# Second layer of a two-layer graph network: counts gathered in pieces and turned by VectorE instead of TensorE, own rows gathered whole, and an edited front

## The reference

```python
h = relu(layernorm(x));  x = x + attention(h, src, dst, W, b_w, a, b_a)
h = relu(layernorm(x))
gates = softmax(h @ gate_W + gate_b);  top_v, top_i = top_k(gates, 2)
def sage_conv(h, W_l, b_l, W_r):
    aggr = segment_sum(h[src], dst) * inv_deg      # mean over a node's neighbours
    return aggr @ W_l + b_l + h @ W_r
for e in range(4):                                  # expert e
    he = relu(sage_conv(h, Wl[e, 0], bl[e, 0], Wr[e, 0]))
    out_e = relu(sage_conv(he, Wl[e, 1], bl[e, 1], Wr[e, 1]))
x = x + sum over the two best experts of gate * out_e
```

## Time and profile before

| | |
|---|---|
| median of 3 runs | 739.95 us (739.89 to 740.51) |
| the profiled execution | 741.92 us, its span 740.2 us |
| TensorE, share of the span | 97% |
| VectorE, ScalarE, GpSimd | 57%, 54%, 26% |
| chain that ended last | TensorE 90%, VectorE 5%, ScalarE 2% |

### The profile page before, as it was taken

How to read it: one execution, slowest core, us unless ns; L and a number is a source line. 1 busy time by engine, 2 the same in 40 slices (tenths; PEclk the granted TensorE clock), 3 DMA queues, 4 the chain that set the end, 5 groups by cost and what they waited for, 6 DMA issues and landing times.

```text
span 740.2 us, 12236 instructions
## 1 busy us (share of the span) xinstructions
PE 720.9 (97%) x3671; PEld 586.5 (79%) x3671; DVE 425.2 (57%) x1052; ACT 398.9 (54%) x898; POOL 191.3 (26%) x207
## 2 busy tenths in 40 slices
PE   7899999999999999999999999989999999999995
PEld 5698977888888888777777777878888888888884
DVE  7989889999752538622722622648345443453541
ACT  8866678776643521511511511347677675687761
POOL 4300000000000101850200010044566467556531
PEclk9999999999999999999999999999999999999998
DMA  9000001111501247799699595379844897327960
GB/s 214 34 4 3 4 3 30 40 35 36 169 4 58 84 125 242 217 334 323 238 354 322 199 363 192 100 191 265 295 93 85 210 292 225 75 73 190 286 203 14
DMA packets 46445, 115.21 MB, mean 156 GB/s; under 512 B 8340, under 2 KB 8552, under 8 KB 46361
## 3 DMA queue, kind: packets, MB, share of 16 engines
q1 hardware_dynamic: 28581, 77.60, 33.0%
q0 software_dynamic: 9136, 19.65, 11.5%
q10 hardware_dynamic: 8644, 16.86, 6.8%
HBM read 64.89 MB, written 50.08 MB: 155 GB/s over the span
## 4 chain that ended last, share of the span: by engine, by line
PE 90%; DVE 5%; ACT 2%; issue 1%; DVEq 0%; POOL 0%; ACTq 0%; POOLq 0%
PE ps L1814 16%; PE ps L1815 16%; PE ps L1816 16%; PE ps L2243 7%; PE ps L2242 6%; PE ps L2043 3%; PE ps L2037 3%; PE ps L2110 3%; PE ps L2111 3%; PE ps L2038 3%; DVE onehot_g L1325 3%; PE ps L1902 2%; PE ps L2173 2%; PE ps L1981 1%; PE ps L1983 1%
## 5 line engine op out<-in xcount | busy, mean ns | idle before, releaser
L1127 ACT ACTIVATE agn<-ps,rec 32x128 f32<-32x128 f32 x336 | 121.1, 361 | 33.3 <-PE ps L2243 18.8
L1055 ACT ACTIVATE slots<-he_t 125x512 fp32r<-125x512 f32 x40 | 25.4, 636 | 150.8 <-DVE he_t L1610 136.0
L2243 PE MATMUL ps<-slots,CTs 125*128 x230 | 90.0, 391 | 0.0
L1610 DVE TENSOR_TENSOR he_t<-ps,b_b 125x512 f32<-125x512 f32 x40 | 27.6, 691 | 105.7 <-PE ps L1816 72.5
L734 POOL DMA_INDIRECT hrow<-t_d,piece_i x80 | 76.1, 951 | 27.1 <-issue 23.8
L2242 PE MATMUL ps<-slots,CTs 125*128 x207 | 80.7, 390 | 0.3 <-issue 0.3
L1814 PE MATMUL ps<-W,agT_hi 128*125 128x512 f32 x160 | 63.5, 397 | 0.0
L1814 PE MATMUL ps<-W,h2T_hi 128*125 128x512 f32 x160 | 63.4, 396 | 0.0
L1816 PE MATMUL ps<-W,agT_lo 128*125 128x512 f32 x160 | 63.3, 396 | 0.0
L1815 PE MATMUL ps<-W,agT_hi 128*125 128x512 f32 x160 | 63.2, 395 | 0.0
L1815 PE MATMUL ps<-W,h2T_hi 128*125 128x512 f32 x160 | 63.2, 395 | 0.0
(11 more groups left out here) (335 smaller groups left out, 1716.8 us busy)
## 6 DMA issues: line engine op xcount, KB each, us to landing
he_d<-slots SPq DMA_DIRECT2D x30, 448.0 KB
slots<-he_d SPq DMA_DIRECT2D x30, 448.0 KB
w_d<-slots SPq DMA_DIRECT2D x3, 4096.0 KB, 17.7
slots<-w_d SPq DMA_DIRECT2D x24, 512.0 KB
t_d<-he_t SPq DMA_DIRECT2D x40, 224.0 KB
raw<-in_L_gnn_Wl ACTq DMA_DIRECT2D x4, 1024.0 KB, 8.9
raw<-in_L_gnn_Wr ACTq DMA_DIRECT2D x4, 1024.0 KB, 5.5
slots<-in_L_gnn_Wl ACTq DMA_DIRECT2D x4, 1024.0 KB, 9.4
```

The lines of the kernel that those rows point to most:

```text
L1127: last = a.activation(agn[32 * r:32 * r + 32, q, :], ps[n, 3 + i % 2, 128 * r:128 * r + 128], ACT.Copy, scale=rec[n, i, 4:5])
L2243: last = mm(o, CTs[:, t, :], part(k, P, t * 1024 + D, P), start=False, stop=t == T - 1)
```

## The change

Second step: the counts are written to `c_d` with permuted columns, 320 for each of four groups (32 nodes of each of ten tiles). `gather_counts` issues four indirect DMAs of 128 x 320 f16 by `piece_i`, and one VectorE transpose (`turn_counts`, 128 x 1,280 f16) puts the turned counts in `cth`; ScalarE copies them to `CTs` (`counts_in`, one instruction; three for tile 1). TensorE's `turn_rows` and VectorE's casts are gone. `gather_hidden` gathers whole rows for every tile, and `turn_hidden` is 16 instructions for every tile but the first. TensorE's turn of tile 0's own rows moves into the middle of `transformed(0)`.

Front: `W0_lo` is made by VectorE in the first batch, the rest of `a_sum` and `s_add` by GpSimd, and VectorE's flags of the second batch are loaded inside `sources`. `ident_a` and the rows 96 to 127 of `ct_16` are filled by GpSimd once the first products are done, and `counts_16(0)` on ScalarE waits for that.

```diff
 def gather_counts(i):                                   # GpSimd
-    gather(crow[i % 3][:], c_d, i, 0, crow_in[i % 3])
+    for q in range(RQ):
+        g.indirect_dma_start(crow[i % 3][:, q, :], None, c_d.rearrange("n (r f) -> (n r) f", r=RQ),
+                             bass.IndirectOffsetOnAxis(ap=piece_i[:, q, i:i + 1], axis=0)
+                             ).then_inc(crow_in[i % 3].sem, 16)
...
 def gather_hidden(i):
-    if i < HB:
-        gather(by_row(hrow[i]), t_d.rearrange("e p t d -> (e p t) d"), i, 1, hrow_in[i])
-        return
-    for q in range(RQ):
-        g.indirect_dma_start(hrow[i % HB][:, q, :], None, t_d.rearrange("e p t (r f) -> (e p t r) f", r=RQ),
...
+    gather(by_row(hrow[i % HB]), t_d.rearrange("e p t d -> (e p t) d"), i, 1, hrow_in[i % HB])
...
+def counts_in(i):                                       # ScalarE
+    if i > 0:
+        act.wait_ge(*agg_done(i))
+    act.wait_ge(*crow_turned(i + 1))
+    for r, n in enumerate(TURNS) if i == 1 else ((0, T),):
+        last = copy(CTs[:, 4 * r:4 * r + n, :], cth[0:P, 4 * r * S:(4 * r + n) * S].rearrange("p (t n) -> p t n", n=S))
...
                 mean_high(i)
+                if i + 2 < NT:
+                    counts_in(i + 2)
                 if i + 1 < NT - 1:
                     mean(i + 1)
...
-def counts_in(i):                                       # VectorE
+def turn_counts(i):
+    dve.wait_ge(*crow_in[i % 3](16 * RQ * (i // 3 + 1)))
     if i > 0:
-        dve.wait_ge(*agg_done(i))
-    for r, n in enumerate(TURNS):
-        dve.wait_ge(*crow_turned(3 * i + r + 1))
-        v.tensor_copy(CTs[:, 4 * r:4 * r + n, :], turned_counts(r, n)).then_inc(cts_ready.sem, 1)
+        dve.wait_ge(*cts_ready(3 * i))
+    v.transpose(cth[:].rearrange("p (t q c) -> p q t c", q=RQ, c=32),
+                crow[i % 3][:].rearrange("p q (t a) -> p q t a", a=32)).then_inc(crow_turned.sem, 1)
...
                 mean_low(i)
                 if i + 2 < NT:
-                    counts_in(i + 2)
+                    turn_counts(i + 2)
                 if i + 1 < NT:
                     turn_hidden(i + 1)
...
-            def turn_rows(i):                           # TensorE
...
-                if i + 2 < NT:
-                    turn_rows(i + 2)
...
+            def first_weights_low():                    # VectorE, in the first batch
+                dve.wait_ge(*w0_hi_ready(1))
+                v.tensor_tensor(W0_lo[:], W0_f[:], f32(W0_hi[:]), ALU.subtract).then_inc(w0_lo_ready.sem, 1)
```

More of the change, by code:

```diff
@@ L236, in gnn_kernel @@
         ag1 = at("ag1", [P, 4, D], F32, R4 + 8192)
[L237 to L241, removed]
+        c_nat = at("c_nat", [P, 2, N], F32, R3 + 21792)
+        ct_16 = [at(f"ct_16_{k}", [128, T, Q], F16, R3 + 4096 + 5024 * k) for k in range(2)]
+        c_16 = at("c_16", [P, 2, RQ * T * 32], F16, R3 + 14144)
+        c_lo = at("c_lo", [P, N], F16, R3 + 19264)
+        ident_a = at("ident_a", [128, 128], F16, R2 + 39328)
         slots = at("slots", [128, 2, 18432], F32R, 0)
@@ L663, in _ @@
                             pool.wait_ge(*ct_out(LOW_OUT, 64 * q + 32 * i))
-                        g.tensor_tensor(c_lo[:], c_nat[:, i, :], c_16[:, i, :], ALU.subtract
-                                        ).then_inc(rest_ready.sem, 1)
+                        low, nat = (o.rearrange("p (t n) -> p t n", n=P) for o in (c_lo[:], c_nat[:, i, :]))
+                        rounded = c_16[:, i, :].rearrange("p (r t a) -> p t r a", r=RQ, a=32)
+                        for r in range(RQ):
+                            m = slice(32 * r, min(32 * r + 32, P))
+                            last = g.tensor_tensor(low[:, :, m], nat[:, :, m], rounded[:, :, r, 0:m.stop - m.start],
+                                                   ALU.subtract)
+                        last.then_inc(rest_ready.sem, 1)
             with pool.If(beyond):
@@ L933, in counts_16 @@
                     act.wait_ge(*c_turned(6 * (q - 1)))
-                copy(ct_16[q % 2][:], CT[:, :, q * Q:(q + 1) * Q]).then_inc(ct_16_ready.sem, 1)
+                if q == 0:
+                    act.wait_ge(*consts(CONSTS + 1))
+                copy(ct_16[q % 2][0:P], CT[:, :, q * Q:(q + 1) * Q]).then_inc(ct_16_ready.sem, 1)
             def root(k, n):
@@ L1313, in tile_and_batch @@
             def tile_and_batch(b):
-                more, before = batch_flags(b) if b > 0 else first_flags
+                more, before = (first_flags, *second_flags)[b] if b < 2 else batch_flags(b)
                 dve.wait_ge(*column_ready(b + 1))
@@ L2161, in half @@
                 return last
-            def turn_rows(i):
-                pe.wait_ge(*crow_in[i % 3](16 * (i // 3 + 1)))
-                if i > 0:
-                    pe.wait_ge(*cts_ready(3 * i))
-                    with pe.If(beyond):
-                        pe.wait_ge(*ctl_ready(3 * i))
-                for r, n in enumerate(TURNS):
-                    for k in range(n):
-                        t = 4 * r + k
-                        last = nc.tensor.transpose(ps_h[0:P, r, k * S:(k + 1) * S], crow[i % 3][:, t * P:(t + 1) * P],
-                                                   ident_h[:])
-                    last.then_inc(crow_turned.sem, 1)
             for x in range(NE):
```

105 lines of the change are left out of this document (56 added, 49 removed).

## The result

The changed kernel takes 776.49 us (median of four executions, 774.61 to 779.5) against 739.92 us for the kernel before: a ratio of 1.0495, 95% interval 1.0478 to 1.0512, so 36.6 us slower. The forecast was 772, in a range from 755 to 786. One of the twelve executions of `front_alone` took 1,442 us, about twice the others; it is in that run's median, but all ratios here compare undisturbed executions only.

A forecast was written before the change was run, and what follows sets the result against it. TensorE bounds the kernel before; afterwards a 12.09 us ring of VectorE and ScalarE does. Rounds 25.8, start 2.2, end 1.1, stalls 4.6, front -1.5 sum to +32.2 us, so 772 us, range 755 to 786.

The forecast's parts named there:

- The ring: Second step: VectorE and ScalarE instructions waiting on each other from one `aggT` to the next, 12.09 us a tile.
- The 19 rounds: Second step, `aggT` of tile 1 to that of tile 20: each round 12.09 us instead of 10.73, +25.8 us.
- TensorE keeps 10.15 us: Second step: TensorE's tile of 10.80 us loses 0.65 with the transposes removed, leaving 10.15.
- TensorE stays the bound: Rival, second step: turn and copy of the counts do not set the pace, so the kernel gets faster, 724.5 us; chance 5%.
- The f16 turn: VectorE's turn of 1,280 count columns takes 1.48 us; the rival had 0.83 at double rate, 760 us in all, chance 10%.
- The clock: Rival: TensorE's clock falls because it idles 1.9 us in each tile, 60 us more, 830 us; chance 4%.
- Sixteen turns hidden: Second step: VectorE's sixteen turns of own rows (5.03 us, not 0.70) lie under copy and `agn` (7.28), costing nothing.
- Start: Second step's beginning: `agn` of tile 1 now follows `heT` of tile 0, `aggT` at 505.65 against 503.45, +2.2 us.
- taken as even: Tile 0: gains 1.95 us from three groups of transposes, loses about as much as TensorE waits for ScalarE's copies.
- Stalls: Second step: two late `agn` starts (idle 4.66 and 3.70 us instead of 1.86) no longer absorbed by slack, +4.6 us.
- Tail: End of second step: `aggT` of tile 20 to that of tile 21 takes 11.50 us instead of 10.41, +1.1.
- Front: First batches: shorter `std` and pauses on VectorE, against `W_lo` added there: -1.5 us, bounds -2.9 and 0.

The follow-up runs named there:

- front_alone: Kernel before with only the front's edits (low first weights to VectorE, bias sum to GpSimd, second batch's flags read earlier): 739.32 us, ratio 0.9988.
- longer_turn: Changed kernel with a second, unused turn of nine tenths of the counts ahead of the real one, from the third later tile on: 802.55 us, ratio 1.0843.
- turn_first: Changed kernel with two VectorE neighbours swapped, the counts turned before the low half of the means: 748.14 us, ratio 1.0100.
- ahead: Changed kernel with VectorE turning the counts one tile earlier, behind the turn of the hidden rows: 736.52 us, ratio 0.9961.
- one_turn: Changed kernel with one whole-block turn for the sixteen small turns of own rows from the third tile on (pieces misplaced): 775.28 us, ratio 1.0466.
- rows_whole: Kernel before with later tiles' own rows gathered whole by one transfer and turned by 16 small VectorE turns: 747.39 us, ratio 1.0093.
- early: Changed kernel with the third tile's counts turned and copied earlier at the start of the second layer: 773.96 us, ratio 1.0459.

## Why the prediction was right, point by point

- **The ring sets the pace.** Forecast 12.09 us, measured 12.16. All terms held within 0.03 us but one: from the turn's start to the copy's 1.62 and not 1.52, the turn itself 1.505 for the assumed 1.48 and the handing over 0.12 and not 0.04. The 19 rounds cost +27.1 us for +25.8. `longer_turn`, `turn_first` and `ahead` each change the ring by one term and give the period that the sum of the others predicts. That this is the cause is shown, not argued.
- **TensorE keeps 10.15 us** when it is let: 10.16 in a tile of `ahead`. The rival "TensorE stays the bound" (724.5) failed only on the order of the program. Its mechanism is real once the turn stands a tile ahead.
- **The f16 turn** takes 1.505 us for 1,280 columns, so 1.05 ns for each of the 768 columns beyond the f32 turn of 512 (0.70), where the sum had 1.02, and far from 0.83 us in all. No double rate: that rival is out. By the Trainium skill, VectorE: DVE Perf Modes, section What auto-detection actually checks, a built-in operation is capped by the modes that firmware enables for it; the trace's 1.505 us fits an operation for which no faster one is enabled.
- **The clock** fell three to five times between 480 us and the last tiles in the two profiles of the changed kernel, as that rival's mechanism has it, but for some us only and in part in other stretches each time. That was worth 1.6 us at the start, not 60.
- **Sixteen turns hidden**: right in the usual steps (`one_turn`). The step from tile 20 to tile 21 has only the copy and eight `agn` over them, about 4.3 us for 5.0; the prediction took the cover of 7.28 for all steps. There they cost 0.6 us in the changed kernel and 2.8 in `rows_whole`.
- **Start**: measured +4.7 with the front's gain in it, for +2.2 - 1.5. Of this 1.6 is a fall of the clock in one execution. The second profile, without that fall, has `aggT` of tile 1 5.0 us later than `front_alone` (506.15 for 501.13). The term +2.2 itself held: from `heT` of tile 0 to that `aggT` are 12.0 us for 9.85. What failed is the step "taken as even", tile 0 itself. ScalarE in `front_alone`, then in the second profile of the changed kernel:

```profile
488.88 0.60 ACT L780 ACTIVATE aggT<-ps 128x512 fp32r<-128x512 f32 x1 [4.18 <-PE ps L2256]
491.28 0.60 ACT L1103 ACTIVATE heT<-ps 128x512 fp32r<-128x512 f32 x1 [1.81 <-PE ps L2263]
```

```profile
490.44 0.60 ACT L787 ACTIVATE aggT<-ps 128x512 fp32r<-128x512 f32 x1 [3.04 <-PE ps L2265]
494.15 0.60 ACT L1129 ACTIVATE heT<-ps 128x512 fp32r<-128x512 f32 x1 [3.11 <-PE ps L2272]
```

  `aggT` is 1.6 us late: TensorE idles 1.54 and 1.53 us before its first two sums, each behind a copy by ScalarE. `heT` is 2.9 us late: the turn of tile 0's own rows, moved into `transformed(0)`, now stands behind six of its matmuls, which take 1.4 us (492.08 to 493.51). No experiment separates the two. `early` wins 3.1 us here, by letting `agn` of tile 1 follow this `heT` at once.
- **Stalls**: +4.6 forecast, 0 measured. The failed step reads, "TensorE had slack for it then; in a ring nothing has". The pauses do not come from the kernel; none of the thirteen later profiles (the changed kernel's and the twelve of the table) has one. One profile was taken for a property of the program.
- **Tail**: +1.1 forecast, +2.7 measured. Tile 20 to 21 is 12.13 for 10.41, +1.7, for 11.50 in the sum; the missing 0.6 are the sixteen turns, without which `one_turn` takes 11.57. The other +1.0 lies behind `aggT` of tile 21; 0.6 of it behind the last `tg` (from 766.27 to the end are 8.4 us, in the kernel before 7.8 from 732.40). It comes again in the second profile, and its cause is open, as `one_turn` has it too (8.5) without the sixteen turns. The rest, 0.3, does not come again (14.60 us from `aggT` of tile 21 to the last `tg`, in the first profile 14.97, in the kernel before 14.65).
- **Front**: -1.5 forecast; alone it measures -1.0 (-0.2 to -1.6). Right in kind.
- The errors of start and front together, stalls and tail nearly cancel (+4.0, -4.6, +1.6), and the rounds add 1.3: 34.5 for 32.2. That the total was nearer than these parts is luck; that it was near at all is the ring's 27.1 of 34.5.

## What to carry to other kernels

When work moves from the full engine to others, don't add it to their busy shares: write down the starts of one round, instruction by instruction, see which wait closes the ring, and compare the ring with the full engine's time. If the ring is longer, look for the operation in it that needs nothing of this round; put it one round ahead, into the pause of its engine, before giving the change up (here 776.5 us became 736.5 by three lines). A pause seen in one profile alone is not a term of a sum until a second profile shows it.

## What the runs showed of the hardware

- VectorE's turn showed no faster rate for f16: 1.505 us for 128x1280 (23 of them, 1.503 to 1.512), 1.37 for 128x1152 in `longer_turn`, against 0.70 for 128x512 in f32.
- TensorE's granted clock can fall towards the lower level behind an idle stretch that in another execution leaves it alone: 1.54 us at 480 us, mean clock 0.71 in the first profile of the changed kernel and 1.00 in the second. Where TensorE is full, the executions with a lower mean clock tended to be the longer ones (734.3 to 740.8 us in `ahead`), which is no proof of a cause; where it has slack inside a ring, three falls cost less than 0.5 us in all (231.27 us for the 19 rounds in the second profile, 231.01 in the first).
- The handing over from VectorE to ScalarE after the large turn took 0.12 us (533.75 + 1.50 to 535.37).
